# Regrouping the tasks of an expert item over its two steps, and the first fill of the ring of expert weights at one item in three quarters

## The reference

```
xn = layernorm(x)
layer 0: x + latent attention(xn)            + low-rank feed-forward(xn)
layer 1: x + gated recurrence over time(xn)  + feed-forward with 4-bit rounding(xn)
layer 2: x + attention(xn)                   + mixture of 32 experts, top 4, width 96,
                                               and a shared expert of width 256
layer 3: x + attention with rotation(xn)     + mixture of 16 experts, top 2, width 256,
                                               with biases, and a shared expert of width 512
```

## Time and profile before

| | |
|---|---|
| median of the runs | 1698.71 us (1696.58 to 1701.24) |
| the profiled execution | 1701.65 us, its span 1699.9 us |
| busy: TensorE, VectorE, ScalarE, GpSimd | 74%, 74%, 54%, 24% of the span |
| mean granted TensorE clock | 0.857 |
| layers 2 and 3 | from about 750 us to the end |

### The profile page before, as it was taken

How to read it: one execution, slowest core, us unless ns; L and a number is a source line. 1 busy time by engine, 2 the same in 40 slices (tenths; PEclk the granted TensorE clock), 3 DMA queues, 4 the chain that set the end, 5 groups by cost and what they waited for, 6 DMA issues and landing times.

```text
span 1699.9 us, 24108 instructions
## 1 busy us (share of the span) xinstructions
PE 1257.0 (74%) x7112; PEld 673.3 (40%) x7198; DVE 1249.4 (74%) x4139; ACT 921.7 (54%) x2172; POOL 413.1 (24%) x578
## 2 busy tenths in 40 slices
PE   6988989887332334256677899977699878989976
PEld 2444544444111112031145566513366344666521
DVE  5988979988789999868655656577767765556562
ACT  3988988886354444412343556544344444545545
POOL 0111202002000000004546345255310054232151
PEclk7989999999755556556789999998899998999989
DMA  3010101100392000012422566333201044446320
GB/s 116 24 70 6 49 27 30 51 0 1 115 326 83 5 6 11 1 44 87 140 72 83 169 187 189 104 86 67 56 31 32 32 137 105 151 126 172 105 68 22
DMA packets 141387, 135.41 MB, mean 80 GB/s; under 512 B 75218, under 2 KB 114455, under 8 KB 141203
## 3 DMA queue, kind: packets, MB, share of 16 engines
q1 hardware_dynamic: 126185, 101.99, 20.2%
q0 software_dynamic: 13440, 31.48, 6.2%
q10 hardware_dynamic: 1632, 0.39, 0.1%
HBM read 95.96 MB, written 47.27 MB: 84 GB/s over the span
## 4 chain that ended last, share of the span: by engine, by line
PE 43%; DVE 37%; issue 7%; ACT 6%; another core or an unknown queue 3%; DMA 2%; POOL 1%; SPq 1%; ACTq 0%; DVEq 0%
PE PS L576 38%; DVE nmx L1487 6%; DVE RA L1732 6%; DVE RA L1736 4%; PE PS L572 4%; DVE RA L1290 4%; DVE RA L1293 3%; DVE RB L1290 1%; PE PS L943 1%; DVE RB L1293 1%; ACT RA L1878 1%; DVE Otok L1217 1%; ACT RA L1928 1%; DVE RA L1455 1%
## 5 line engine op out<-in xcount | busy, mean ns | idle before, releaser
L576 PE MATMUL PS<-RA 128*128 128x512 bf16 (+6 forms) x1963 | 505.7, 354 | 104.6 <-DVE nmx L1487 69.1
L1487 DVE TENSOR_REDUCE nmx<-PS 128x1 f32<-128x512 f32 x512 | 347.6, 686 | 235.9 <-PE PS L576 204.3
L1928 ACT ACTIVATE RA<-PS 128x512 f32<-128x512 f32 x512 | 295.7, 598 | 261.6 <-PE PS L576 183.0
L576 PEld LDWEIGHTS PS<-RA 128*128 128x128 bf16 (+4 forms) x2048 | 193.9, 122 | 367.2 <-DVE nmx L1487 148.5
L576 PE MATMUL PS<-RA,Vs 128*32 128x512 f32 x1240 | 205.2, 657 | 3.5 <-ACT RA L1928 1.0
L2054 ACT ACTIVATE RA<-RA 128x8 f32<-128x8 f32 x511 | 107.5, 210 | 142.9 <-DVE RA L1732 142.7
L572 PE MATMUL PS<-ident,RB 128*128 128x128 f32 (+2 forms) x331 | 61.8, 330 | 158.5 <-DVE RB L1665 142.9
L1290 DVE TENSOR_SCALAR RA<-PS 128x1024 f32<-128x1024 f32 x96 | 117.0, 1219 | 19.6 <-PE PS L576 18.9
L1878 ACT ACTIVATE RA<-RA,nm 128x512 f32<-128x512 f32 x192 | 128.8, 725 | 1.1 <-POOL nm L2224 0.9
L1293 DVE CUSTOM_DVE_ANT_0 RA<-RA,RB 128x512 f32<-128x512 f32 x192 | 125.1, 689 | 3.3
L572 PE MATMUL PS<-ident,RA 128*128 128x128 f32 x768 | 107.1, 284 | 26.5 <-ACT RA L1884 17.7
(11 more groups left out here) (312 smaller groups left out, 2124.3 us busy)
## 6 DMA issues: line engine op xcount, KB each, us to landing
RA<-scr SPq DMA_DIRECT2D x288, 96.0 KB
RA<-wd SPq DMA_DIRECT2D x28, 384.0 KB
xd<-Otok SPq DMA_DIRECT2D x36, 256.0 KB, 3.3
RA<-xd POOLq DMA_DIRECT2D x72, 128.0 KB, 3.7
RA<-wd SPq DMA_DIRECT2D x56, 160.0 KB
RB<-wd SPq DMA_DIRECT2D x20, 384.0 KB
RB<-wd SPq DMA_DIRECT2D x40, 160.0 KB
scr<-parts SPq DMA_DIRECT2D x48, 128.0 KB
```

The lines of the kernel that those rows point to most:

```text
L576: return e.matmul(o, l, r, start=first, stop=last)
L1487: e.tensor_reduce(nmx[:, (g + lx) % 3, c:c + 1], bank[(6, 0)[i % 2]], AX.X, ALU.max, negate=True).then_inc(*ROWMAX.up(layer, n, i))
L1928: e.activation(chunk(layer, k, i), bank[(1, 5)[i % 2]], ACT.Exp).then_inc(*EXP.up(layer, k, i))
```

## The change

The two steps of an item get other tasks. Before, one step holds `rows`, `turned(i+2)`, `hidden(i+1)` and `down(i)`, the other `gated(i+1)` and `address(i+2)`. After, one step holds `rows` and `hidden(i+1)`, the other `down(i)`, `turned(i+2)`, `gated(i+1)` and `address(i+2)`, in this order. The number of steps, and so the quarters on which they fall, stays. The first fill of the ring of weights is done at one piece a quarter in both layers (before: two a quarter in layer 3), and only every third piece loads an item.

```diff
             if i >= first:
-                steps.append(fetch + ([("turned", i + 2)] if nsh <= i + 2 < end else []) + ([("hidden", i + 1)] if i + 1 < end else []) + [("down", i)])
-            steps.append(([("gated", i + 1)] if i + 1 < end else []) + coming)
+                steps.append(fetch + ([("hidden", i + 1)] if i + 1 < end else []))
+            steps.append(([("down", i)] if i >= first else []) + ([("turned", i + 2)] if i >= first and nsh <= i + 2 < end else [])
+                         + ([("gated", i + 1)] if i + 1 < end else []) + coming)
@@ step of SyncE
             at_ = 4 * n + i - ROUTE_LATE[layer] - LOAD_FROM
-            for piece in range(at_, at_ + 1) if lx == 0 else range(2 * at_, 2 * at_ + 2):
-                weights(lx, piece)
+            weights(lx, at_)
@@ weights
-            if i in range(3, 3 + ahead[lx]):
-                item_weights(lx, len(shared[lx]) + i - 3)
+            if i % 3 == 0 and 0 < i <= 3 * ahead[lx]:
+                item_weights(lx, len(shared[lx]) + i // 3 - 1)
```

## The result

The changed kernel takes 1691.73 us (median of 9 runs, 1688.68 to 1695.01), the kernel before 1698.71 in the 9 runs beside it. The ratio is 0.9967, with a 95% interval of 0.9951 to 0.9983: 3 to 8 us faster, a small but resolved gain. The forecast was 1699 us and no change. The time lies inside the range of 1683 to 1713, but the sign was missed.

A forecast was written before the change was run, and what follows sets the result against it. TensorE was taken as the bound in the four item stretches, 39 us idle. Terms -16 + 23 + 0.5 - 3.5 - 3 - 2 + 3 = +2 us gave 1703.7, lowered for a slow profiled execution and cautious rounding to 1699 us; range 1683 to 1713.

The forecast's parts named there:

- Step 3: Turned rows behind the down product: bank 2 waits shrink, 3.5 us back; layer 2's first-fetch stall gets work, 3 us back.
- Step 2: Turned rows nearer their inner product: TensorE waits for ScalarE's copy in both layers, 23 us lost, between 8 and 38.
- Step 1: Down product leaves the inner product's step in both layers: its wait for gating goes, 16 us back, between 9 and 23.
- the first fetch: TensorE's 5.23 us stall before layer 2's turned(16): other products run inside it, 3 us back, between 0 and 4.
- the long waits: Four of the down product's 20 gating waits, 10.1 us together, VectorE late: half counted, 5 us back, bounds 0 and 10.1.
- B: Rival, faster, 1684 us: TensorE may run two quarters ahead of VectorE, waits go, the copy costs only 12; chance 0.25.
- A: Rival, slower, 1711 us: ScalarE's copy replaces gating as the wait at 74 of 96 items; chance 0.23.
- The bank: Banks 3 and 4, shared by inner and down products: ScalarE's evacuation copy, 0.37 us, stays covered by other work; nothing charged.
- Step 4: Ring fill spread out: 2 us back in layer 2, 3 us lost in layer 3 to a delayed row-maximum transfer.
- TensorE's idle time: Test over the four item stretches: the prediction is wrong if idle moves from 39 us by more than 6.
- C: Rival, 1706 us: layer 3's fills delay the row-maximum transfer by 4 us or more, steps 1 to 3 cancel; chance 0.07.
- D: Rival, 1699 us: lists move, but TensorE's order costs the same wherever it stands; chance 0.05.

The follow-up runs named there:

- e8: The kernel before with ten useless TensorE products ahead of the first routed turned rows of layer 2; 1695.95 us, ratio 0.9989.
- e7: The changed kernel with turned rows behind hidden(i+1) in its step, except the first routed ones of layer 2; 1679.48 us, ratio 0.9908.
- e5: The kernel before with only down(i) moved to the other step, in both layers; 1685.24 us, ratio 0.9925.
- e9: The kernel before with down(i) moved in both layers and only layer 2's first routed turned rows one step later; 1679.45 us, ratio 0.9912.
- e10: The kernel before with down(i) and the first routed turned rows moved in layer 2 only, layer 3 left alone; 1676.88 us, ratio 0.9905.
- e3: The kernel before with only turned(16), the first routed item of layer 2, one step later; 1689.2 us, ratio 0.997.
- e1: The changed kernel's steps with the ring fill of the kernel before; 1687.26 us, ratio 0.9959 of the kernel before.
- e6: The kernel before with only turned(i+2) moved to the other step, down(i) left in place; 1707.19 us, ratio 1.0062.
- e2: The kernel before with only the change's ring fill, steps as before; 1694.42 us, ratio 1.0003.

## Why the prediction was wrong, step by step

The mechanisms were there, nearly all of them; the sum came out at +2 us where 7 were won. Step 3 was too small in both of its terms, by far, and a mechanism in it was missing, the clock behind a stall. Step 2's price shows only together with what bank 2 gives back, and there some 8 to 10 us stand where 19.5 were forecast. Step 1 was right in total and wrongly spread.

**Step 3, what turned rows stop waiting for: this is the step that failed.** For the first fetch it said "3 us back, between 0 and 4". Three quarters became 6.0 us shorter (4 to 6 over all kernels). The part that I had seen, work that runs inside the stall, was right in size (3.4 by e8). The part that I hadn't is the clock: 2.6 us by e8, because TensorE came out of 5.2 us of idleness at the lower level. The group stood before me with the stall, and the transposes in the same row take 0.66 us where the earlier trace rows has 0.38 for the same pair: the low clock could be read there. I had taken the granted clock of whole stretches (0.97 to 0.99), whose borders left this place out. "TensorE: Matmul & The Clock Gate", section What's actually happening, in the Trainium skill says that the array idles at 1.2 GHz and only activity lifts that; these rows agree.

For bank 2 it said 3.5 us back, "between 0 and 5": seven waits of line 1217, 0.5 us of each. Of the 9.1 us of this line 0.6 are left, and with the other readers of the bank 17.3 us in 20 waits became 0.8 in 4. I had left out the other rows, the wait of 2.41 us at 1503.83 among them, and the low clock behind that one. Those eight quarters became 4.6 us shorter, and layer 3 came out even by it. How much time each of the other waits gave back isn't shown, since every run that ends them brings other waits with it (for the turned copy, in e7 for the down copy).

**Step 1, down leaves the inner product's step: right in kind and in total, too small in layer 2, too large in layer 3.** The gating waits went as forecast (16.1 to 1.8, forecast under 6). In the routed stretch of layer 2 I had 6.2 us and the long waits' share; e5, e9 and e10 give 11.2, 11.0 and 11.1 (9.4 to 9.6 against e3, whose clock is equal). The discount "0.17 of each 0.24" for overlapping records was the error: undiscounted, the exposed loads of the earlier trace rows are 9.3, and PE's busy time, which I took as a floor ("can win back no more than parts of the 39 us"), held the rest. The shared items gained about 2 us on the mean of all kernels, against 3.4. For layer 3 I had 1.4 and a part of the long waits; e10 against e9 shows none. In all some 13 us came, where 16 were forecast.

**Step 2, turned rows a step nearer: right in kind; its 23 us can't be weighed apart from bank 2.** Together with the 3.5 us of bank 2 it stood at +19.5. In layer 2 the stretch of the changed kernel stands 9.4 us above e9's (173.0 and 163.6), e1, with e9's fill but a clock of 1.00 against 0.99, 7.7 above, and e6 7.6 above before. In layer 3 the changed kernel is at 183.0 against e9's 182.6: 4 to 5 us lost over the stretch and 4 to 5 won in quarters 410 to 418. So about 8 to 10 us in all stand against 19.5, and the difference is of the size of the bank 2 waits that went beyond the 3.5. The waits for line 1914 came out as described (45 of 0.33 on average, forecast 40 to 90 of 0.2 to 0.4). The thresholds that I set (under 10 for B, over 25 for A) put 14.8 between both. In e6, where down stays, layer 3 took 189.6. Its trace has both prices: of the gating waits 11.0 us are left and of the bank 2 waits 8.8, and the waits for the turned copy are 18.6 us in 50 times.

**The bank, charged with 0: wrong by itself, hidden in the sum.** The trace of e7 agrees with the rule of the Trainium skill ("Perfetto Trace Analysis", section Optimizing Tensor Performance) that I had weighed and set aside: with down moved and nothing but score products in between, the loads wait for the down copy 17.7 us in 30 times (3.3 in 7 in e9), and layer 2 takes 5.2 us more (168.8 against 163.6; 3.2 us of waits for the turned copy are in that too). In the changed kernel this wait lies under the one for the turned copy, which is longer since both copies stand on ScalarE one behind the other. "Two banks in turn" wasn't enough; what counts is what TensorE has to do between the two uses of one bank. The upper bound of 38 us had this queue in it, and I took the middle.

**Step 4, the fill:** -2 and +3 were forecast, 0 within 5 us was found (e2).

**TensorE's idle time** in the four stretches was to stay within 6 of 39 us; over the same quarters it is 33.6 after (869 to 915.5, 923.4 to 1096.8, 1210.6 to 1306.8, 1420.7 to 1604 us). It stayed within by a hair, and it is a poor measure, as e5 shows: in the routed stretch of layer 2, a third of the gain was idle time, and two thirds left the busy column.

**The rivals.** A (slower) named the true cost but at 23 to 25 us against 10 to 13, without the bank 2 waits that would go; in layer 2 it is 9.4 against 11.1. B (faster, 1684) had the right sign, and in part for its reason (the waits of step 3 count for more than I gave them), but TensorE's waits for reductions stayed (64.6 us now, 69.1 before), so no decoupling from VectorE was won. C is refuted. D is refuted by e5 and e6: in layer 2, order takes 11 us off or adds 8. My sum by the measured terms would be -4 to -6 for the first fetch, -1.6 to -3.3 for the routed items of layer 2 (the changed kernel and e1), about -2 for the shared ones and 0 for layer 3 and the fill: -8 to -11 us. The median moved by 7.0 us (3 to 8), and other segments' differences between executions, up to 2 us each, can cover the rest.

**What stays open:** how the return of the bank 2 waits and the price of the copy divide the difference in step 2, and why the row-maximum transfer takes from 2.7 to 10.3 us from kernel to kernel. No run separates these.

## What to carry to other kernels

Lay a count of some instruction that occurs once in each step over the traces of both kernels, and compare lengths between equal counts: that finds gains of 6 and 5 us at two places which busy totals don't show. A stretch that comes out even can hold a gain and a loss. A stall in front of a transfer or of a bank that is still being read costs TensorE its idle time and the low clock behind it, so put work whose data are there ahead of the first use of such data, even if everywhere else the other order is better. Before a task is moved, list every wait that it has now and not only the largest row: the ones that go are part of the price. When a task is moved closer to its consumer, price the consumer by all the copies that queue on the evacuating engine, and look for what stands between two uses of the same bank; if a change is a gain and a loss in one (-11 and +9 here), do the half that gains.

## What the runs showed of the hardware

After 5.2 us without a matmul the granted clock was 0.50 to 0.55 for about 6 us, and eight products took 1.92 us instead of 1.06; with useless products in the gap it was 1.00 and they took 1.06. Shorter gaps went both ways: behind a wait of 2.41 us (before, 1503.83) and one of 1.86 us (e5, 1560.20) it was 0.51 (the lower level, 1.2 GHz) for 3.4 us, while in the changed kernel waits of 1.06 and 0.93 us around 920 us and one of 2.0 us at 1417.2 left it at 1.00. A transfer of 12 KB took 2.7 to 10.3 us at the same place of kernels that differ in the order of tasks and in the fill. Three kernels with the same order in the routed stretch of layer 2 agreed within 0.2 us there (163.4, 163.6, 163.5); four with before's order lie within 2.7 us (173.0 to 175.7) and three with the change's within 1.7 (171.3 to 173.0). How repeatable a segment is has to be seen for each.
